# Reading a 48-row tile with all 128 rows in the down projection of a decoder block

## The reference, cut to what matters

```python
scores = jax.nn.softmax(xf @ w_router.T, axis=-1)
topk_w, topk_idx = jax.lax.top_k(scores, K)                 # K = 2 of 8 experts
topk_w = topk_w / (topk_w.sum(axis=-1, keepdims=True) + 1e-20)
cw = (jax.nn.one_hot(topk_idx, E, dtype=xf.dtype) * topk_w[..., None]).sum(axis=1)
g = jnp.einsum('th,ehi->tei', xf, wg)
u = jnp.einsum('th,ehi->tei', xf, wu)
eo = jnp.einsum('tei,eih->teh', jax.nn.silu(g) * u, wd)     # the down projection
y = jnp.einsum('te,teh->th', cw, eo)
y = y + jax.nn.silu(xf @ wg_s) * (xf @ wu_s) @ wd_s         # the shared expert
```

## Time and profile before

| | |
|---|---|
| median of 3 runs | 1901.47 us (1900.26 to 1901.95) |
| span of the profiled execution, first to last instruction | 1896.3 us |
| its own time beside the span | not listed apart; the median is 5.2 us above the span |
| TensorE busy | 1679.0 us, 89% |
| GpSimd busy | 1548.3 us, 82% |
| VectorE busy | 1504.8 us, 79% |
| ScalarE busy | 1421.6 us, 75% |
| mean granted TensorE clock | 0.952 |
| instructions | 25668 |

### The profile page before, as it was taken

How to read it: one execution, slowest core, us unless ns; L and a number is a source line. 1 busy time by engine, 2 the same in 40 slices (tenths; PEclk the granted TensorE clock), 3 DMA queues, 4 the chain that set the end, 5 groups by cost and what they waited for, 6 DMA issues and landing times. The chain is left out here.

```text
span 1896.3 us, 25668 instructions
## 1 busy us (share of the span) xinstructions
PE 1679.0 (89%) x7046; PEld 960.4 (51%) x7046; DVE 1504.8 (79%) x1890; ACT 1421.6 (75%) x4402; POOL 1548.3 (82%) x1284
## 2 busy tenths in 40 slices
PE   4678999999899999989999998999999899998976
PEld 1234454656545465654646565464655545465544
DVE  4888878888897888988788888879888897878332
ACT  5479687786978778797887869788787978767362
POOL 0678888989898888988888898888889898898734
PEclk7679999999999999999999999999999999999988
DMA  2312312222221212322121233212223321231102
GB/s 97 90 39 79 95 49 85 64 68 101 79 95 51 84 62 68 101 79 94 48 89 62 68 101 79 94 49 88 62 68 101 79 95 49 77 96 49 62 3 65
DMA packets 125918, 140.43 MB, mean 74 GB/s; under 512 B 44048, under 2 KB 69456, under 8 KB 125776
## 3 DMA queue, kind: packets, MB, share of 16 engines
q1 hardware_dynamic: 125776, 138.79, 24.4%
HBM read 133.77 MB, written 4.98 MB: 73 GB/s over the span
## 5 line engine op out<-in xcount | busy, mean ns | idle before, releaser
L1171 POOL TENSOR_TENSOR prod<-state,c_rep 128x1024 f32<-128x1024 f32 x256 | 610.0, 2385 | 36.7 <-PE p_y L629 18.7
L1034 DVE TENSOR_TENSOR_SCAN state<-decay,p_drive 128x1024 f32<-128x1024 f32 x256 | 584.6, 2284 | 26.1 <-ACT decay L771 12.8
L771 ACT ACTIVATE decay<-delta,a_neg 128x504 f32<-128x504 f32 x512 | 360.1, 721 | 51.8 <-DVE state L1034 50.5
L629 PE MATMUL p_y<-prod,ident 128*128 128x512 f32 x768 | 397.3, 610 | 0.0
L1024 DVE TENSOR_TENSOR p_drive<-u,p_drive 128x1024 f32<-128x1024 f32 x256 | 312.7, 1221 | 66.7 <-PE p_drive L617 66.4
L903 ACT ACTIVATE ex<-p_ring,nmax 128x64 f32<-128x64 f32 x1024 | 307.4, 368 | 2.9 <-DVE nmax L1086 2.3
L903 ACT ACTIVATION_READ_ACCUMULATOR ex<-p_ring,nmax 128x1 f32 x1024 | 253.7, 262 | 0.0
L729 PE MATMUL p_ring<-x2T,wg 128*128 128x512 f32 x416 | 234.6, 665 | 3.6 <-ACT us L955 3.6
L729 PE MATMUL p_ring<-x2T,wu 128*128 128x512 f32 x384 | 200.8, 621 | 31.8 <-DVE km L1145 19.4
L1224 POOL TENSOR_TENSOR ex<-ex,rden 128x512 f32<-128x512 f32 x128 | 144.9, 1132 | 81.0 <-DVE rden L1090 80.7
L943 ACT ACTIVATE gt<-p_ring 128x512 f32<-128x512 f32 (+1 forms) x208 | 123.8, 596 | 116.3 <-PE p_ring L729 113.1
(11 more groups left out here) (141 smaller groups left out, 3110.5 us busy)
## 6 DMA issues: line engine op xcount, KB each, us to landing
c_rep<-c_rows SPq DMA_DIRECT2D x256, 256.0 KB, 3.6
cwr<-cw_rows SPq DMA_DIRECT2D x64, 256.0 KB, 3.4
ctxT<-in_ctx_t SPq DMA_DIRECT2D x32, 256.0 KB, 5.5
cwr<-cw_rows SPq DMA_DIRECT2D x32, 224.0 KB, 2.9
cwr<-cw_rows SPq DMA_DIRECT2D x32, 192.0 KB, 2.8
cwr<-cw_rows SPq DMA_DIRECT2D x32, 160.0 KB, 3.0
xf<-in_x SPq DMA_DIRECT2D x16, 256.0 KB, 4.4
xb<-in_x SPq DMA_DIRECT2D x16, 256.0 KB, 4.7
```

What stands on the lines that cost most here:

```text
L629: pe.matmul(p_y[1 - first][:], ident[:], prod[:, slot_of(c, n), 1 - first, :], start=False, stop=n == STATE - 1, skip_group_check=True).th ...
L771: act.activation(decay[:, n % 2, j, :].rearrange("p (b t) -> p b t", t=SEQ)[:, :, 1:], delta[:, c.parity, j, :].rearrange("p (b t) -> p b ...
L1034: dve.tensor_tensor_scan(state[:, slot_of(c, n), :, :].rearrange("p j t -> p (j t)"), decay[:, n % 2, :, :].rearrange("p j t -> p (j t)"), ...
L1171: pool.tensor_tensor(mine, state[:, slot_of(c, n), :, :], c_rep[:, n % C_SLOTS, :].unsqueeze(1).to_broadcast([128, HALVES, T]), ALU.mult). ...
```

## The change

The products of the thirteenth tile read all 128 rows of acts[12] and of the last tile of wd. So that the unused 80 rows of acts[12] hold zeros, VectorE fills the whole tile once in the prologue. The number and the order of TensorE's instructions stay the same; VectorE has one instruction more.

```diff
@@ -744,10 +744,9 @@
                                 pe.wait_ge(gu_ready.sem, gu_ready.at(c.m, ON_POOL.index(SPLIT)))
                             elif i == 0 and g == 0 and j >= ROUTED:
                                 emptied(pe, "up_u", j, c.m)
-                            rows = slice(0, REST if j == SPLIT else 128)
                             mm = pe.matmul(p[:, g * D:(g + 1) * D],
-                                           acts[j][rows, (2 * i + g) * 128:(2 * i + g + 1) * 128],
-                                           wd[rows, j, :], start=False, stop=j == FFN_TILES - 1)
+                                           acts[j][:, (2 * i + g) * 128:(2 * i + g + 1) * 128],
+                                           wd[:, j, :], start=False, stop=j == FFN_TILES - 1)
                 mm.then_inc(ring_full[r].sem, 1)
 
             turns("pe", step)
@@ -996,6 +995,7 @@
             dve.tensor_scalar(a_neg[:].rearrange("p a n -> p (a n)"), a_neg[:].rearrange("p a n -> p (a n)"),
                               -1.0, None, ALU.mult).then_inc(consts_v.sem, 1)
             dve.memset(decay[:], 0.0)
+            dve.memset(acts[SPLIT], 0.0)
             dve.memset(vm[:], 0.0)
             dve.memset(r_sel[:, :, EXPERTS:], TOP_EPS)
             dve.memset(r_cw[:], 0.0).then_inc(consts_v.sem, 1)
```

## The result

The changed kernel takes 1874.03 us (median of 4 runs, 1873.60 to 1876.38) against 1900.87 for the kernel before in the same measurement: a ratio of 0.9862, 95% interval 0.9848 to 0.9876. A repetition later gave 0.9847 (0.9833 to 0.9862). The profiled span went from 1896.3 to 1871.5 us, 24.8 less; the difference of the medians, 26.8, is larger because the profiled execution of before was some 3 us quicker than its median: in timed runs about 2 us lie around the span, not 5.

What follows compares the result with a forecast made beforehand. TensorE's down step was taken as the bound, the other engines waiting for it. Span 1896.3 - 24.0 (products) + 0.4 (GpSimd) + 0.5 (fill) = 1873.2 us, plus 5.2 around it: 1878.4 us, range 1865 to 1891.

Steps and rivals of the forecast that it cites:

- The excess of 0.39 us per product, read from starts and not from busy means: Down projection: each 48-row product costs 0.39 us more than one of 128; removing this saves 24.0 us in all.
- The rival by busy sums: Down projection: only busy time goes, 128 records x 45 ns = 5.8 us, less 0.5, giving 1896.2 us; chance 0.04.
- Zeros cost as much as numbers: Thirteenth tile's products: reading 80 rows of zeros takes 0.112 us per record, like the other twelve tiles.
- GpSimd is the next to be late: Before the first score product: GpSimd's km becomes later than ScalarE's by some 0.03 us, costing 0.4 us over 14 turns.
- The fill: Prologue: VectorE's one zero fill of 128x512 delays the start by 0.5 us, nothing at best and 0.6 at most.
- The clock keeps its share of long falls: TensorE's drops to 1.2 GHz: about five of twelve turns stay long; otherwise 8 us less or 11 us more.
- a rival of its own in all turns at once: Thin routing stage: the clock stops falling, a turn saves another 1.7 us, giving about 1856 us; chance 0.03.
- The start of the sum: Whole kernel: profiled span of 1896.3 us, with the median 5.2 us above it taken as time around the span.
- The slower rival: Attention scores: the clock falls a second time per turn, up to 3.4 us each, 1932 us in all 16; chance 0.02.

Runs made afterwards that it cites:

- km shared four and four: The changed kernel with one of GpSimd's five products of km moved to ScalarE: 1879.68 us, 0.9881 of the kernel before.
- dt: Step-size product (L665, 64 rows) padded with zero weights to 128 rows: 1857.35 us on the changed kernel, 1877.14 us on the kernel before.
- twice the short tiles: The kernel before with the sixth tile also read over only 48 rows, leaving 80 of its rows out: 1909.77 us, ratio 1.0078.

## Why the prediction was right, and where not, point by point

The time lay in the range (1874.0, forecast 1878.4, 1865 to 1891) and the mechanism was the one forecast; two terms of the sum were off in size and in opposite directions. That 1873.2 us of span were forecast and 1871.5 measured is in part luck: in the twelve turns the products gave 3.7 us less than I had (14.1 for 17.8), and the clock gave 5.9 that I had not put in.

- *The excess of 0.39 us per product, read from starts and not from busy means.* Right: 1.41 us less from the down step to L682, and 0.10 on it, 1.51 as worked out. The rival by busy sums (1896.2) fell. The excess is 0.39 us per product at 48 and at 64 rows, and nothing at 96. The Trainium skill's statement that the count of rows doesn't matter to a weight load ("TensorE: Matmul & The Clock Gate", Part 2, step 1) thus doesn't give the time of a product among neighbours of another form. What fits is a sentence of another page of the Trainium skill, "TensorEngine Tiling (Array Packing)", Key Properties: a change of tiling mode drains the engine. No run here shows in which mode a product ran, so that this is the reason is not shown. The page gives no price; the runs give 0.39 us for in and out at 128 columns of fp32, paid once for two products side by side.
- *Zeros cost as much as numbers.* Right; ten records take 1.12 us.
- *GpSimd is the next to be late.* Right in kind, too small in size, and this is the first term that was mis-sized. I let L1215 come 0.97 us earlier; it came 0.86 (14.77 to 13.91 us into the turn). I had given GpSimd the whole 0.73 of the first half, but its statistics wait for the end of the last product of that half, and part of the excess lies behind that end, on the transposes: GpSimd's row came 0.58 us earlier in the turn (911.20 - 903.31 = 7.89, 896.86 - 889.55 = 7.31). GpSimd's km then ended 0.14 us behind ScalarE's (907.19 and 907.05), and the score came 1.24 us earlier, not 1.48. That is half of the 0.24 us missing. The other half is a cost that the sum did not have: the score starts 0.26 us behind the end of GpSimd's km (907.19 to 907.45), where it started 0.14 behind the end of ScalarE's before (922.31 to 922.45), and 0.15 with km shared four and four, where ScalarE's is the later again (914.71 to 914.86). The km 4 and 4 run shows that this meeting sets the turn. At the mix of before a turn is 1.18 us shorter: over twelve turns 14.1 us, where I had 17.8.
- *The fill.* I took 0.5, at most 0.6; hpad came 0.8 us later, since the whole prologue of VectorE also began 0.26 us later (the fill of decay at 9.83, 9.57 before). The 2.61 us in the earlier trace rows are how long ScalarE had waited when hpad began, not how far hpad lay behind the fill, which ended 0.04 us before it. In the time it doesn't show (1.0008).
- *The clock keeps its share of long falls.* Wrong, the second term: 5 of 12 long before, 4 after with 3 turns without any, 5.9 us of the 24.8. The range had room for it (8 us less at best), but the way I had drawn it, between short and long alone, missed that the fall can stay away. I held that for a rival of its own in all turns at once (0.03); it came in a quarter of them. The ends of the range don't quite come out of its own terms either: 1878.4 less 8 and 3 is 1867, and with 11 and 3 it is 1892, where I put 1865 and 1891.
- *The start of the sum.* The 5.2 us around the span were in fact about 2, the rest a quick execution; a sum made on a single profile inherits that.
- The slower rival, a second fall in the turn at the scores, was not seen in the changed kernel: no turn of the twelve has more than 6.83 us at the low clock.

Still open is why the mix moves as it does. In two profiled executions of the changed kernel it was alike, and it does not go one way with the length of the turn: 111 us with twice the short tiles has five turns of twelve without a fall, 110 us before has none, 109.23 has a short one in each.

## What to carry to other kernels

Read the cost of a row of products from start to start, and include the instruction behind it: the busy means showed 45 ns of what was 0.2 us per record. A lone product over 48 or 64 rows in a run of full ones was worth padding with zeros to 96 or 128 rows where its time lay on the path, or, where that can't be, putting side by side with another of its kind. (For dt the padding gave no gain in turns of like clock.) And compare turns of like clock before taking a difference of totals for the price of an edit: here the clock made a quarter of one gain and most of another, and in twelve turns it took 11 of 18 us off one loss.

## What the runs showed of the hardware that was not expected

- A change between 128 and 48 or 64 rows costs 0.39 us for in and out at 2.4 GHz and 128 columns of fp32, the same for one product or two in between; 96 rows cost nothing.
- TensorE's clock can fall to 1.2 GHz in every turn of one kernel, for 3.4 or 6.8 us, and stay at 2.4 GHz in two thirds of the turns of another with the same work but one kind of product over more rows; a turn differs by 0.9 to 1.5 us between none and a short fall, and by 1.6 to 1.7 between a short and a long one.
- The clock can also stay at 1.2 GHz while products follow one another without a pause: for 28.29 us at the end of the profiled execution with twice the short tiles. In the kernel before it rose 5.52 us into the same products.
- TensorE's first score product starts 0.26 us behind the end of GpSimd's work when it waits for that, and 0.14 to 0.15 behind the end of ScalarE's.
